# A spectral step and a graph convolution over one 4096 x 4096 matrix: stage 1's loads by two rows and 1,024 columns instead of four rows and 512

## The reference

```python
def reference(x, adj, evals, t, W, b):
    spec = adj.T @ x
    y = adj @ (exp(-evals * max(t, 1e-8))[:, None] * spec)
    x = layernorm(x + y)
    a = adj + eye(4096)
    a = a / a.sum(axis=1, keepdims=True)
    y = tanh(a @ (x @ W) + b)
    return layernorm(x + y)
```

## Time and profile before

| | us |
|---|---|
| median of 3 runs | 629.96 (629.28 to 630.16) |
| profiled execution: device time | 632.82 |
| profiled execution: span of the instructions | 630.7 |
| busy: PE, DVE, ACT, POOL | 590.4, 515.1, 396.3, 364.4 |
| mean granted TensorE clock | 0.983 of full |
| HBM read, written | 172.13 MB, 2.11 MB |

### The profile page before, as it was taken

How to read it: one execution, slowest core, us unless ns; L and a number is a source line. 1 busy time by engine, 2 the same in 40 slices (tenths; PEclk the granted TensorE clock), 3 DMA queues, 4 the chain that set the end, 5 groups by cost and what they waited for, 6 DMA issues and landing times.

```text
span 630.7 us, 8071 instructions
## 1 busy us (share of the span) xinstructions
PE 590.4 (94%) x2486; PEld 451.3 (72%) x2486; DVE 515.1 (82%) x604; ACT 396.3 (63%) x859; POOL 364.4 (58%) x206
## 2 busy tenths in 40 slices
PE   6999999999996789999999999999999969999992
PEld 5878788778774566667888888888888847655561
DVE  4789989988887999698879889596776576989992
ACT  4899999999986644545565655545443454445552
POOL 0000000000131988877999999778886779796961
PEclk9999999999999799999999999999999989999997
DMA  8999999999999999999987999298994499999201
GB/s 285 386 387 386 386 387 387 387 387 387 386 331 328 280 301 252 287 266 272 317 220 198 263 280 302 60 264 204 247 251 133 128 346 296 345 332 296 58 18 50
DMA packets 141305, 174.67 MB, mean 277 GB/s; under 512 B 6868, under 2 KB 105428, under 8 KB 141272
## 3 DMA queue, kind: packets, MB, share of 16 engines
q1 hardware_dynamic: 88992, 121.68, 61.3%
q10 hardware_dynamic: 52280, 52.58, 30.6%
HBM read 172.13 MB, written 2.11 MB: 276 GB/s over the span
## 4 chain that ended last, share of the span: by engine, by line
PE 69%; POOL 9%; DVE 6%; ACT 5%; DMA 4%; issue 3%; SPq 1%; ACTq 1%; POOLq 0%; DVEq 0%
PE ps L759 13%; PE ps L761 13%; PE ps L760 13%; PE ps L735 7%; POOL lo L409 7%; PE ps L736 6%; PE ps L737 6%; PE ps L755 6%; DMA raw<-in_adj_dram 4%; ACT hi L445 3%; DVE vt L596 3%; PE ps L824 1%; PE ps L827 1%; POOL rstd L401 1%; ACT hi L460 1%
## 5 line engine op out<-in xcount | busy, mean ns | idle before, releaser
L409 POOL TENSOR_TENSOR lo<-vt,hi 128x1024 fp32r<-128x1024 f32 x129 | 326.7, 2559 | 59.1 <-ACT hi L460 58.2
L596 DVE STREAM_TRANSPOSE vt<-raw 128x1024 f32<-128x1024 f32 x184 | 222.2, 1226 | 62.9 <-PE ps L761 52.4
L460 ACT ACTIVATE hi<-vt 128x1024 fp32r<-128x1024 f32 x163 | 169.6, 1061 | 111.3 <-DVE vt L596 93.1
L579 DVE TENSOR_TENSOR lo<-raw,hi 128x1024 fp32r<-128x1024 f32 x124 | 153.5, 1240 | 21.3 <-ACT hi L445 20.7
L445 ACT ACTIVATE hi<-raw 128x512 fp32r<-128x512 f32 x256 | 158.2, 621 | 14.2 <-DMA raw<-in_adj_dram 4.8
L391 POOL TENSOR_TENSOR lo<-raw,hi 128x1024 fp32r<-128x1024 f32 x4 | 10.7, 2685 | 180.8 <-ACT hi L445 180.8
L759 PE MATMUL ps<-hi,s_hi 128*128 128x512 f32 x232 | 99.1, 427 | 9.5 <-issue 5.2
L735 PE MATMUL ps<-hi,xg_hi 128*128 128x512 f32 x256 | 102.0, 399 | 2.7 <-DVE lo L579 1.4
L736 PE MATMUL ps<-lo,xg_hi 128*128 128x512 f32 x256 | 99.9, 390 | 0.0
L737 PE MATMUL ps<-hi,xg_lo 128*128 128x512 f32 x256 | 99.8, 390 | 0.0
L759 PE MATMUL ps<-hi,p_hi 128*128 128x512 f32 x206 | 89.1, 433 | 7.0 <-POOL lo L409 7.0
(11 more groups left out here) (66 smaller groups left out, 512.9 us busy)
## 6 DMA issues: line engine op xcount, KB each, us to landing
raw<-in_adj_dram SPq DMA_DIRECT2D x63, 1024.0 KB, 14.2
raw<-in_adj_dram SPq DMA_DIRECT2D x90, 512.0 KB, 9.3
raw<-in_adj_dram ACTq DMA_DIRECT2D x88, 512.0 KB, 11.6
late_raw<-in_adj_dram SPq DMA_DIRECT2D x8, 512.0 KB, 11.6
late_raw<-in_adj_dram ACTq DMA_DIRECT2D x8, 512.0 KB, 14.3
xn<-in_x_dram SPq DMA_DIRECT2D x8, 256.0 KB, 12.2
x_sb<-in_x_dram SPq DMA_DIRECT2D x8, 256.0 KB, 13.1
out_dram<-x_sb ACTq DMA_DIRECT2D x8, 256.0 KB, 3.0
```

The source lines that it names most:

```text
L409: nc.gpsimd.tensor_tensor(lo[:, slot(p), :], vt[:, slot(p), :], hi[:, slot(p), :].bitcast(f32), ALU.subtract).then_inc(pool_lo_ready, 1)
L460: nc.scalar.activation(hi[:, slot(s), :], vt[:, slot(s), :], ACT.Copy).then_inc(hi_ready, 1)
L579: nc.vector.tensor_tensor(lo[:, q % RING1, :], raw[:, k, 2 * h:2 * h + 2, :].rearrange("p r n -> p (r n)"), hi[:, q % RING1, :].bitcast(f3 ...
L596: nc.vector.transpose(vt[:, slot(s), :].rearrange("p (m a i) -> p m a i", m=2, a=RB), load_buffer(st.load).rearrange("p (a m e i) -> p e m ...
```

## The change

A chunk is now two rows a partition and 1,024 columns, still 1 MB in the same buffer. Chunks k = 2u and 2u + 1 are the first and the last two of the four rows a partition, over the column range of the banks 2u and 2u + 1. A row's piece is one run of 4 KB in the source and in the buffer. A half h is now one row of 1,024 columns: ACT makes its two pieces of 512, whose row sums go to the columns of `rsum` that belong to that row and those banks, DVE or POOL one subtraction of 1,024 as before. PE makes the same six matmuls a half, three into bank 2u and three into bank 2u + 1, now with the x of one row as weights. The sums of both banks are complete with chunk 2u + 1, so DVE's copies of a pair stand together, at odd i. The first chunk is still loaded in two DMAs of 512 KB, now a row each.

```diff
--- before.py
+++ after.py
@@ -26,6 +26,7 @@
 
 
 def spectral_then_graph_conv(nc, x, adj, evals, t, W, b, out):
+
 
 
 
@@ -178,7 +179,7 @@
     def slot(s):
         return (s + RING1) % RING
 
-    adj_x = adj.rearrange("(g p r) (k w) -> g k p r w", r=R, p=P, w=CW)
+    adj_x = adj.rearrange("(g p h r) (u w) -> g u h p r w", h=2, r=R // 2, p=P, w=2 * CW)
     x_n = x.rearrange("(g p r) c -> g p (r c)", p=P, r=R)
     adj_q = adj.rearrange("(v a e n) (u q w) -> v e u q n a w", v=NU, e=2, n=QP, q=QN, w=WQ)
     x_v = x.rearrange("(u a e h r) c -> u e a h (r c)", u=NU, e=2, h=QP // R, r=R)
@@ -332,7 +333,7 @@
                 if freed is not None:
                     sp.compute_val(src.offset * 4)
                     sp.wait_ge(freed, count)
-                sp.dma_start(raw[:, k], src).then_inc(raw_in[k], 16)
+                sp.dma_start(raw[:, k].rearrange("p (r e) w -> p r (e w)", e=2), src).then_inc(raw_in[k], 16)
 
             def load_xn(v, par):
                 sp.dma_start(xn[:, par, :], x_n[v]).then_inc(xn_in[par], 16)
@@ -340,17 +341,18 @@
             def visit1(v, par, v_index):
 
                 for k in range(NK):
-                    load1(adj_x[v_index, k], k, lo1_ready, (v - 1) * PAIRS + (2 * k + 2))
+                    load1(adj_x[v_index, k // 2, k % 2], k, lo1_ready, (v - 1) * PAIRS + (2 * k + 2))
                     if k == 3 and par is not None:
                         sp.wait_ge(x_ready, v)
                         load_xn(v_index + 1, par)
 
             load_xn(0, 0)
-            sp.dma_start(raw[:, 0, :R // 2], adj_x[0, 0][:, :R // 2]).then_inc(first_in, 16)
-            sp.dma_start(raw[:, 0, R // 2:], adj_x[0, 0][:, R // 2:]).then_inc(raw_in[0], 16)
+            for r, signal in enumerate((first_in, raw_in[0])):
+                sp.dma_start(raw[:, 0, 2 * r:2 * r + 2].rearrange("p e w -> p (e w)"), adj_x[0, 0, 0][:, r])\
+                    .then_inc(signal, 16)
             for k in range(NK):
                 if k:
-                    load1(adj_x[0, k], k)
+                    load1(adj_x[0, k // 2, k % 2], k)
                 if k == 3:
                     load_xn(1, 1)
             with sp.Fori(0, NU - 1) as d:
@@ -441,10 +443,11 @@
                     q = 2 * k + h
                     if not (isinstance(v, int) and v == 0 and q < RING1):
                         act.wait_ge(mm1_done, PAIRS * v + (q - RING1 + 1))
-                    for r in (2 * h, 2 * h + 1):
-                        last = nc.scalar.activation(hi[:, q % RING1, (r % 2) * CW:(r % 2 + 1) * CW],
-                                                    raw[:, k, r, :], ACT.Copy,
-                                                    accum_out=rsum[:, v, r * NK + k:r * NK + k + 1])
+                    r = 2 * (k % 2) + h
+                    for e in range(2):
+                        column = r * NK + 2 * (k // 2) + e
+                        last = nc.scalar.activation(hi[:, q % RING1, e * CW:(e + 1) * CW], raw[:, k, 2 * h + e, :],
+                                                    ACT.Copy, accum_out=rsum[:, v, column:column + 1])
                     last.then_inc(hi1_ready, 1)
 
             def visit1(v, par, next_count):
@@ -615,8 +618,9 @@
                 for h in range(2):
                     if i < NK and 2 * i + h in LATE_DVE:
                         half1(LAST, i, h)
-                if 0 <= (k := i - 2) < NK:
-                    dve.wait_ge(mm1_done, PAIRS * LAST + 2 * k + 2)
+
+                for k in ((i - 3, i - 2) if i % 2 == 1 and 0 <= i - 3 < NK else ()):
+                    dve.wait_ge(mm1_done, PAIRS * LAST + 4 * (k // 2) + 4)
                     u = k // 2
                     if u >= 2:
                         dve.wait_ge(sT_done, u - 1)
@@ -729,12 +733,14 @@
                         wait_lo1(pe, q)
                     else:
                         pe.wait_ge(lo1_ready, PAIRS * v + (q + 1))
-                    for r in (2 * h, 2 * h + 1):
-                        xh, xl = (a[:, par, r * C:(r + 1) * C] for a in (xg_hi, xg_lo))
-                        ah, al = (a[:, q % RING1, (r % 2) * CW:(r % 2 + 1) * CW] for a in (hi, lo))
-                        nc.tensor.matmul(ps[:, k, :], xh, ah, start=first and r == 0, stop=False)
-                        nc.tensor.matmul(ps[:, k, :], xh, al, start=False, stop=False)
-                        last = nc.tensor.matmul(ps[:, k, :], xl, ah, start=False, stop=final and r == R - 1)
+                    r = 2 * (k % 2) + h
+                    xh, xl = (a[:, par, r * C:(r + 1) * C] for a in (xg_hi, xg_lo))
+                    for e in range(2):
+                        bank = ps[:, 2 * (k // 2) + e, :]
+                        ah, al = (a[:, q % RING1, e * CW:(e + 1) * CW] for a in (hi, lo))
+                        nc.tensor.matmul(bank, xh, ah, start=first and r == 0, stop=False)
+                        nc.tensor.matmul(bank, xh, al, start=False, stop=False)
+                        last = nc.tensor.matmul(bank, xl, ah, start=False, stop=final and r == R - 1)
                     last.then_inc(mm1_done, 1)
 
             def visit1(v, par, first=False):
```

## The result

The changed kernel takes 625.97 us (median of 5 runs, 625.81 to 627.59) beside 630.16 us for the kernel before on the same chip (5 runs, 629.28 to 631.64). The ratio is 0.9937, 95% interval 0.9919 to 0.9956. That is 4.2 us less, with an interval of 2.8 to 5.1. The profiled execution took 627.59 us, the highest of the five, with a span of 625.4 us.

A forecast was written before the change was run, and what follows sets the result against it. DMA bounds stage 1, with PE 0.6 us behind in each 22.36 us group; faster transfers make PE the bound. Sum: -5.3 + 0.7 = -4.6 us, span 626.1, median 625.4 us, range 624.0 to 628.6 us.

The forecast's parts named there:

- What bounds stage 1: Stage 1 before the change: DMA is the bound, with PE 0.6 us behind it in each group of 22.36 us.
- Term 1: Stage 1's transfers: runs of 4 KB for 2 KB raise the rate from 387 to 409 GB/s; bounds 387 and 433.
- Term 2: PE from its first product to spectrum 0: 5.5 us are waits, of which 5.3 us are saved; bounds 0 and 5.5.
- What I said would be seen in the queue: Stage 1's load queue: DMA share under 1, issue to landing from 14.2 to under 10 us, average 395 to 400 GB/s.
- Term 3: Spectra at stage 1's end: DVE's paired copies delay the last pair and stage 2's first product, +0.7 us; bounds 0.66 and 2.0.
- hidden as well: DVE's half of lo behind the second copy pair: ends 0.66 us later, hidden because the next half waits for POOL anyway.
- The pass-through to the end: From stage 2's loads on: engines set the pace, one transfer wait of 1.5 us between 198 and 300 us; gain reaches the end.
- (a): Stage 1's transfers: runs of 4 KB are no faster than 387 GB/s, only the 0.7 us cost stays, 630.6 us; chance 0.12.
- (b): Stage 1: rate ends between 387 and 398 GB/s, DMA stays the bound, or ACT falls behind; 628.0 us; chance 0.11.
- (c): No faster transfers, and DVE's doubled copies run late, costing PE 0.66 us three times, 2.0 us in all: 632.0 us; chance 0.05.

## Why the prediction was right, and where it was not

The forecast was 625.4 us (624.0 to 628.6); the two medians of the change are 625.97 and 626.80. Direction, size and bound are as forecast. Point by point:

**What bounds stage 1: right.** DMA did, with PE 0.6 us a group behind it. With 2 KB in the changed kernel the 22.36 us come back, with 8 KB the 21.76 stay.

**Term 1, the transfers: right.** 409 GB/s was the value of the sum and is the value measured. The estimate by the 3 cycles a packet of the Trainium skill (DMA: Bandwidth & Descriptors, section Why small descriptors are slow) was 396 GB/s, and the runs don't bear it out: the fixed part here is 9.1 ns over four sizes, a quarter of what a kilobyte takes. The 358 GB/s for a core that the Trainium skill gives (the same page, section Specifications) are passed with runs of 2, 4 and 8 KB (387, 409 and 421 GB/s), with one core working alone.

**Term 2, what PE gets: nearly.** Spectrum 0 came 4.87 us earlier for 5.3. PE's first product stood 0.1 us later, and about 0.5 us of waits are left between the two, for 0.2. The waits that the profile still shows for PE there are two for POOL's lo, 0.7 us at its weight loads: they close less far than I had worked out. What I said would be seen in the queue was wrong, though it costs nothing: DMA share 1.03 and 15.4 us from issue to landing, for under 1 and under 10. A group's transfers need 21.15 us for PE's 21.76, so the loads win 0.6 us a group and some 4 us over the stage, less than the reserve of eight buffers. The queue never ran empty and stood at 409 GB/s from end to end, not at 395 to 400.

**Term 3, the passage: the step that failed.** I had 0.7 us, with 2.0 as the upper bound; it took 2.2 (4.87 less 2.68), in three parts of 0.66, 0.66 and 0.88 us. Its one counted part, banks 6 and 7 behind the `s_lo` of 200.28, measured 0.66 us (4.23 to 3.57) as worked out. Two more stand beside it:

- "hidden as well" was wrong for the half behind the second pair. It is true that PE waits for POOL there, and POOL starts no later behind spectrum 0 than before (8.22 us, for 8.21). But the half of lo that DVE made 0.66 us later then ran into POOL's: DVE from 185.56, POOL from 185.58, and POOL's subtraction of 2.39 us took 3.44 (2.78 before, with DVE's half starting 0.68 us ahead of it). The same happened the other way at 176.56, where DVE started 0.31 us behind POOL and took 3.15 us for 1.22: it ended 1.1 us after POOL did. The difference between the two profiles in POOL's duration, 0.66 us, is the loss between spectrum 0 and spectrum 2; with the copies elsewhere it went away. The Trainium skill has the rule, which the prediction left out (SBUF — State Buffer, section SBUF: two separate sides): a DVE operation with two inputs from SBUF and a GpSimd one that reads SBUF lock a shared pair of ports against each other for a whole instruction. These rows agree: the second one's end is the first one's end plus its own usual duration, within 0.2 us. At 176.56 it cost the last chain nothing, as PE would have waited at the next half in any case.
- The transposes of spectrum 3 took 1.97 us for 1.09, a term that the prediction put at nothing. The granted clock there is 0.50 (1.2 GHz); before, it was still 1.00 (2.4 GHz), as the windows show, of the change and of the kernel before:

```profile
198.70:201.00 2.30, 1.83 (x8) 1.43 (x8) 1.99 (x5) 0.43 (x2) 0.00 (x0) 0.50 1.13 206
```

```profile
202.00:203.00 1.00, 0.87 (x8) 0.85 (x8) 1.00 (x5) 0.00 (x0) 0.00 (x0) 1.00 1.13 294
```

PE had been idle for 4.23 us before them, 3.57 in the kernel before. The longer idle time isn't the whole story: in the kernel with 8 KB it is the same and the transposes took 1.09 us, nearly all at the higher level:

```profile
197.93 1.09 PE L755 MATMUL ps<-ident,spec 128*128 128x128 f32 x8 [4.23 <-DVE spec L629]
```

```profile
198.00:199.00 1.00, 1.00 (x8) 0.79 (x8) 1.00 (x5) 0.00 (x0) 0.00 (x0) 0.97 1.14 259
```

There the passage cost 1.3 us and not 2.2 (stage 2's first product 27.5 us behind spectrum 0), which is the 0.88 us. In both profiles of the change and in that with 2 KB the transposes took 1.97 us, with 1 KB 1.80, all behind the same 4.23 us. What sets the moment is open; not asking for the clock in front of a short stretch of PE work behind an idle one was the omission.

**The pass-through to the end: right, and the first profile misleading.** From stage 2's first product to the end nothing changed. But the first profile of the kernel before has 2.8 us in that part that no other profile has, which filled the gap that term 3 left. By the profiles with 419 us the change is worth 2.7 to 3.0 us, by the medians 3.7 to 4.2, by the interval 2.8 to 5.1. A microsecond between them isn't settled. The clock is a likely part of it: the five executions of the change with a mean clock of 0.979 or 0.980, both profiled ones among them, have spans of 624.5 to 626.0 us, and the six at 0.982 to 0.984 have 623.4 to 624.3, so the 0.88 us may well be lost in some executions only. This isn't shown, since the mean over an execution doesn't say where the clock fell, and with 2 KB the spans don't divide by it. PE's first product alone moves between 12.45 and 13.90 us from profile to profile, and where PE is the bound that goes straight through.

**Luck.** The number fits better than the sum. By the first pair of profiles terms 2 and 3 together give 2.7 us at stage 2's start and not 4.6: 0.4 us too much was put on the one and 1.5 too little on the other. That the median still came within 0.6 to 1.4 us of 625.4 is in part luck.

**The rivals.** (a) fell with the 1 KB and the 2 KB kernel. (b) didn't come, since the rate passed 398 GB/s. (c)'s mechanism, DVE's doubled copies being late, did happen in one of its two places, through POOL and not through PE, at 0.66 us, on top of a gain and not of none.

## What to carry to other kernels

Where a queue stays full, two run lengths in one trace give the fixed part of a run, and with it the rate at a third; then look for the next engine's pace, because the gain ends there. When work moves on DVE, look at who works beside it: an instruction of 1.2 us that starts a moment after POOL's can last as long as both. Where PE has a short stretch of work behind an idle one, read its granted clock. And take a second profile before explaining a difference far behind the change.

## What was not expected of the hardware

- Each run costs 9.1 ns beside its 37.8 ns a kilobyte on each of 16 engines, from 1 KB to 8 KB, to about 1 ns, while the queue is full. At 1 KB the rate was the same 349 GB/s with one queue and 128 partitions a load as with two queues and 32 partitions.
- Two subtractions, one on DVE and one on POOL, both from SBUF, that overlap by their starts are served one after the other: 3.15 us for 1.22 on DVE, 3.44 for 2.39 on POOL.
- The same transposes of spectrum 3, after the same copies, behind the same 4.23 us of idle time, took 1.97 us in three profiles (granted clock 0.50), 1.80 in a fourth and 1.09 in a fifth (0.97).
